# First layer of a four-layer graph stack: two fp32 products become three rounded passes each, with their inputs split by ScalarE and VectorE

## The chip, the cores and the metric

The kernel runs on one core of one Trainium2 chip. The metric is the device time of one execution in microseconds; the kernel before has a median of 2340.16 us over 3 runs (2339.61 to 2341.25).

## The reference

Input `x` is 128 graphs of 64 nodes with 256 features, 8192 token rows; `adj` is one 64 x 64 matrix that all graphs share. Four graph layers follow one another, each as `x = layernorm(x + layer(x, adj))`. The change touches the first. For it the reference, cut to its arithmetic, is:

```python
z  = (2 / lambda_max * L - I) @ x          # mixes the 64 nodes of a graph
h  = layernorm(z @ Wc + bc, g1, be1)
x1 = x + relu(h)
q, k, v = x1 @ Wq, x1 @ Wk, x1 @ Wv        # 4 heads of 64
a  = softmax(where(adj > 0, q @ k.T / 8, -1e9))
x2 = layernorm(x1 + (a @ v) @ Wo + bo, g2, be2)
m  = gelu(x2 @ W1 + b1) @ W2 + b2
x  = layernorm(x + layernorm(x2 + m, g3, be3))
```

The first product is `z @ Wc`, the output product `(a @ v) @ Wo`, both 256 x 256 weights.

## The kernel before, in words

The first layer runs over 32 groups of 256 token rows (`GROUP`), each as two tiles of 128 rows. Four groups are under way at once, the streams s0 to s3 (`STREAMS`); each stream has two PSUM banks, in two halves, and its own buffers. Each stream takes 8 turns, a new group each.

The work on a group is cut into numbered slots, each on one or several engines. In the texts here **s2.4** is slot 4 of stream 2. What the slots are, with the line of the trace that shows them:

- 0: TensorE mixes the nodes (L864, 4 matmuls of fp32, 128 columns); ScalarE copies the result out of PSUM as fp32 (L720).
- 1: TensorE's first product with Wc (L829, 4 fp32 matmuls of 256 columns, which a trace shows as 8 records); VectorE adds the bias (L777) and takes layernorm statistics (L319, L323); GpSimd makes the reciprocal root (L331, L333).
- 2: VectorE normalizes (L361 twice, L366 twice), and makes x1 (L784).
- 3: TensorE transposes x1 (L852), ScalarE writes its rounded upper part (`fm[s][:, 0]`, type fp32r, L723), VectorE the rest, the difference (`fm[s][:, 1]`, L767). This pair of instructions is a split.
- 4, 5: TensorE's products for q, k and v. Each fp32 product is made of three rounded passes (`exact_mm`, L298): upper by upper, rest by upper, upper by rest; 24 passes in slot 4, 12 in slot 5. ScalarE copies the results out (L726, L727, L730).
- 6: TensorE's scores (L883, L893), VectorE's maximum (L788). 7: ScalarE's exponentials (L734). 8: VectorE's sum and division (L792, L794, L796). 9: TensorE transposes (L900), ScalarE copies (L739). 10: attention by values (L911), ScalarE's copy (L742).
- 11: the output product with Wo (L829), VectorE's sum (L801) and statistics. 12: VectorE normalizes (L361, L366). 13: transposes, ScalarE's upper part (L746), VectorE's split (L767). 14: TensorE's 24 passes with W1; ScalarE's gelu (L750).
- 15: product with W2 (L829, 8 fp32 matmuls), VectorE's sum (L810) and statistics. 16: VectorE normalizes. 17: statistics for the last layernorm. 18: ScalarE applies it (L351). GpSimd adds on 512-element rows in 3, 13 and 16 (L703, L707, L711).

Every engine works through its queue in the order in which its instructions are written. That order comes from a table by hand, `plan0`: per engine and slot a tick. A turn of a stream starts `lead[s]` ticks earlier than that of stream 0, and a round is 88 ticks; `weave` goes through the ticks of a round and, at equal ticks, through the streams in order. Ticks only order the work, they are no times. The round is unrolled at both ends and stands in a loop between them. In one round every slot of every stream is done once, each at its own turn.

The layer is preceded by a setup, in which ScalarE and GpSimd also split the weights that the passes use (L505, L499), while VectorE and TensorE square a matrix of 64 x 64 step by step to find its largest eigenvalue. All engines meet at a barrier behind the setup, and again behind the layer.

Of the kernel before, what the change touches and what calls it, by code (L numbers as in the profile page):

```python
# [21 lines left out]
ALU = mybir.AluOpType  # L22
# [100 lines left out]
def build_program(nc, ctx, t, out_rows):  # L123
# [485 lines left out]
    xr0, zt_words, hbuf, x1, vt, x1b, x2b = ([buf(G2) for _ in S] for _ in range(7))  # L609
# [5 lines left out]
    zT_f = [blocks_of(v) for v in zt_words]  # L615
# [43 lines left out]
    with nc.Block() as block:  # L659
# [98 lines left out]
        def _(dve):  # L758
# [65 lines left out]
        def _(pe):  # L824
# [7 lines left out]

            def product_by_graph(out, src, w):
# [974 lines left out]
```

## Time and profile before

| | us |
|---|---|
| median of 3 runs | 2340.16 |
| profiled execution | 2342.6 |
| its span, first to last instruction | 2340.7 |
| first layer, first to last of its matmuls | 42.4 to 674.2 |
| one round of the first layer | 78.40 |

The page gives shares over the whole program, of which the first layer is a quarter; what bounds it is read in stretches and timelines of that layer. Since one round is like the next, one of them is shown, from s2.4 at 219.24 us to s2.4 at 297.66 us. A row of a timeline merges instructions of one line that follow one another. The rows are in the section ahead of the prediction.

### The profile page before, as it was taken

Reading aid. Unit: us, or ns where it says so; the run is one execution under the profiler, and the core shown is the slowest. Engines: PE = TensorE matmul, PEld = TensorE weight load, DVE = VectorE, ACT = ScalarE, POOL = GpSimd, SP = SyncE. Lnnn points to the kernel's source line nnn. Section 1 sums busy time; section 2 is a strip of 40 time slices with the busy share of each in tenths; the row PEclk is TensorE's granted clock in tenths of the full one; section 3 lists DMA queues with packets and bytes.
Section 4 is the critical chain, followed back from the end, with each engine's and each line's share of the span. In section 5 each row is a group of like instructions: output and inputs, shape, how many; then the busy total and the mean of one; then the engine's idle time right before and its main releaser. Section 6 shows DMA issues by size and latency. Waiting matters only on the chain. (4 is left out here: it accounts for less than half of the span.)

```text
span 2340.7 us, 39332 instructions
## 1 busy us (share of the span) xinstructions
PE 2172.1 (93%) x14671; PEld 1939.7 (83%) x14671; DVE 1391.9 (59%) x2733; ACT 1206.5 (52%) x2295; POOL 480.1 (21%) x905
## 2 busy tenths in 40 slices
PE   5999999999969989999999999999998897979997
PEld 3888888888859988888888889988887897968886
DVE  3788778877855645443334433444433787857776
ACT  1453455345523347644444434444433566958887
POOL 3344334433430000000000000000000221016665
PEclk9999999999979999999999999999999898989999
DMA  2110111011122101000000000000000331012221
GB/s 97 33 55 18 40 49 54 18 40 49 37 82 63 54 30 36 1 18 1 1 1 19 19 1 1 1 1 1 1 1 18 107 109 54 0 32 64 72 72 50
DMA packets 76397, 81.77 MB, mean 35 GB/s; under 512 B 6545, under 2 KB 74001, under 8 KB 75409
## 3 DMA queue, kind: packets, MB, share of 16 engines
q1 hardware_dynamic: 76304, 80.51, 10.9%
q8 instruction: 62, 1.02, 0.2%
q14 instruction: 31, 0.25, 0.0%
HBM read 55.33 MB, written 25.17 MB: 34 GB/s over the span
## 5 line engine op out<-in xcount | busy, mean ns | idle before, releaser
L298 PE MATMUL ps<-R 128*128 128x256 f32 (+3 forms) x8520 | 1490.9, 335 | 38.2 <-DVE R L1506 14.2
L298 PEld LDWEIGHTS ps<-R 128*128 128x128 f32 x8520 | 1326.6, 190 | 183.2 <-DVE R L767 14.8
L1200 ACT ACTIVATE late_half<-ps,lstm_bias 128x512 f32<-128x512 f32 (+2 forms) x460 | 283.0, 669 | 383.0 <-PE ps L298 382.9
L340 POOL TENSOR_TENSOR ln_veps<-ln_mv,eps_tile 128x2 f32<-128x2 f32 x128 | 28.4, 222 | 1283.0 <-DVE ln_mv L323 1283.0
L829 PE MATMUL ps<-H 128*128 128x256 f32 x1024 | 237.6, 381 | 3.0 <-ACT H L750 1.7
L829 PEld LDWEIGHTS ps<-H 128*128 128x128 f32 x1024 | 189.0, 191 | 26.1 <-ACT H L750 1.9
L1235 DVE TENSOR_TENSOR late_half<-late_half 128x1024 f32<-128x1024 f32 (+2 forms) x32 | 37.6, 1175 | 186.8 <-ACT late_half L1200 186.8
L1197 ACT ACTIVATE late_half<-late_half 128x1024 f32<-128x1024 f32 (+2 forms) x66 | 68.1, 1031 | 124.4 <-DVE late_half L1240 78.4
L1237 DVE TENSOR_TENSOR late_half<-late_half 128x1024 f32<-128x1024 f32 (+2 forms) x32 | 37.6, 1175 | 132.6 <-ACT late_half L1200 132.6
L366 DVE SCALAR_TENSOR_TENSOR H<-H,ln_rstd 128x256 f32<-128x256 f32 x192 | 106.5, 596 | 6.7 <-POOL ln_rstd L333 3.2
L319 DVE BATCH_NORM_STATS2 ln_stats<-H 128x6 f32<-128x256 f32 x256 | 95.9, 416 | 5.3 <-POOL H L711 2.0
L1244 DVE TENSOR_TENSOR H<-late_half 128x1024 f32<-128x1024 f32 (+2 forms) x34 | 45.8, 1348 | 89.2 <-ACT late_half L1200 89.2
L1219 DVE TENSOR_TENSOR R<-H,R 128x1024 fp32r<-128x1024 f32 (+2 forms) x66 | 95.6, 1450 | 1.3 <-ACT R L1180 1.1
L343 POOL TENSOR_TENSOR ln_rstd<-ln_veps,minus_half 128x2 f32<-128x2 f32 x128 | 92.9, 726 | 10.0
L1180 ACT ACTIVATE R<-H 128x1024 fp32r<-128x1024 f32 (+2 forms) x66 | 94.4, 1432 | 0.0
L361 DVE SCALAR_TENSOR_TENSOR H<-H,ln_mv 128x256 f32<-128x256 f32 x192 | 90.6, 512 | 2.2 <-issue 1.8
L1247 DVE TENSOR_TENSOR late_half<-late_half 128x1024 f32<-128x1024 f32 (+2 forms) x32 | 37.6, 1176 | 81.1 <-ACT late_half L1200 81.1
L750 ACT ACTIVATE H<-ps,b_col 128x256 f32<-128x256 f32 x128 | 50.2, 474 | 66.1 <-PE ps L298 66.1
L1025 PE MATMUL ps<-adjT,H 128*128 128x128 f32 x512 | 61.0, 281 | 21.4 <-DMA H<-residual 21.4
L1025 PEld LDWEIGHTS ps<-adjT,H 128*128 128x128 f32 x512 | 60.2, 198 | 21.7 <-issue 21.7
L323 DVE BATCH_NORM_AGGREGATE ln_mv<-ln_stats 128x2 f32<-128x6 f32 x448 | 56.0, 166 | 35.2 <-DVE ln_stats L319 27.9
L331 POOL TENSOR_TENSOR ln_veps<-ln_mv,eps_tile 128x2 f32<-128x2 f32 x96 | 21.5, 224 | 268.9 <-DVE ln_mv L323 268.9
(208 smaller groups left out, 2860.6 us busy)
## 6 DMA issues: line engine op xcount, KB each, us to landing
H<-in_x SPq DMA_DIRECT2D x64, 256.0 KB, 4.1
residual<-H SPq DMA_DIRECT2D x32, 256.0 KB, 2.2
H<-residual SPq DMA_DIRECT2D x32, 256.0 KB, 2.9
arena<-residual SPq DMA_DIRECT2D x32, 256.0 KB, 2.7
residual<-arena SPq DMA_DIRECT2D x32, 256.0 KB, 2.2
H_state<-residual SPq DMA_DIRECT2D x32, 256.0 KB, 2.7
out<-H_state SPq DMA_DIRECT2D x32, 256.0 KB, 2.2
arena<-in_wih SPq DMA_DIRECT2D x4, 1024.0 KB, 5.0
```

What stands on the lines that cost most here:

```text
L298: mm = pe.matmul(out, lhsT(a), rhs(b), start=start and n == 0, stop=stop and n == len(PASSES) - 1)
L319: c.step(dve.bn_stats(ln_stats[:, s, n, :], y[:, n, :]))
L323: ins = dve.bn_aggr(ln_mv[:, s, n, :], ln_stats[:, s, n, :])
L343: c.step(pool.tensor_tensor(ln_rstd[:, s, :], ln_veps[:, s, :], minus_half[:, 0:TILES], ALU.pow))
L361: c.step(dve.scalar_tensor_tensor(out=y[:, n, :], in0=y[:, n, :], scalar=ln_mv[:, s, n, 0:1], in1=g, op0=ALU.subtract, op1=ALU.mult))
L366: ins = dve.scalar_tensor_tensor(out=y[:, n, :], in0=y[:, n, :], scalar=ln_rstd[:, s, n:n + 1], in1=be, op0=ALU.mult, op1=ALU.add)
L829: mm = pe.matmul(out[:, n, :], src[:, k, n * P:(n + 1) * P], w[:, k, :], start=(k == 0), stop=(k == blocks - 1))
L1025: mm = pe.matmul(out[:, k, n * P:(n + 1) * P], src[:, n, k * P:(k + 1) * P], adjT[:], start=True, stop=True)
L1180: act.activation(x.as_window(xin[x.s][:, 0]), x.window(), ACT.Copy).then_inc(x_hi[x.s], 1)
L1197: act.activation(x.part(bg), x.part(cell[s]), ACT.Tanh).then_inc(tanh_ready[s], 1)
L1200: ins = act.activation(into[q][:, m, 0:x.cols], gate_ps(q, m, x.cols), ACT.Tanh if q == TANH_G else ACT.Sigmoid, bias=lstm_bias[:, x.p - 1 ...
L1219: dve.tensor_tensor(x.as_window(xin[x.s][:, 1]), x.window(), x.as_window(raw(xin[x.s][:, 0])), ALU.subtract).then_inc(x_ready[x.s], 1)
```

## The change

- The weights Wc and Wo get split copies `Wc_r` and `Wo_r` in `R`; the setup splits six weights instead of four.
- The buffers for the fp32 copies (`zt_words`, `zT_f`) go. In slots 0 and 10 ScalarE writes the upper part into `fm[s][:, 0]`, the pair that slots 3 and 13 use, and VectorE makes the rest. So VectorE has four splits for a group instead of two.
- The products of slots 1 and 11 are `exact_product`: per product 12 passes instead of 4 fp32 matmuls. The product with W2 in slot 15 stays in fp32.
- Slots 1 and 11 wait for the split (`fm_ready`) instead of the copy.
- In `plan0` VectorE gets ticks for slots 0 and 10, and several ticks move by one or two.

```diff
-    splits0 = ((Wq_r, Wq), (Wk_r, Wk), (Wv_r, Wv), (W1_r, W1))
+    splits0 = ((Wc_r, Wc), (Wq_r, Wq), (Wk_r, Wk), (Wv_r, Wv), (W1_r, W1), (Wo_r, Wo))
...
-    FM = 2
+    FM = 4
     plan0 = dict(
         period=88, lead=(0, 13, 19, 31),
-        pe={0: 15, 1: 19, 3: 31, 4: 36, 5: 41, 6: 46, 9: 60, 10: 65, 11: 70, 13: 80, 14: 86, 15: 93},
-        act={0: 18, 3: 34, 4: 39, 5: 44, 7: 54, 9: 64, 10: 67, 13: 81, 14: 89, 18: 122},
-        dve={1: 26, 2: 31, 3: 35, 6: 51, 8: 60, 11: 77, 12: 80, 13: 85, 15: 100, 16: 104, 17: 111},
+        pe={0: 13, 1: 19, 3: 31, 4: 36, 5: 41, 6: 46, 9: 60, 10: 64, 11: 71, 13: 81, 14: 87, 15: 94},
+        act={0: 15, 3: 34, 4: 39, 5: 44, 7: 54, 9: 63, 10: 66, 13: 82, 14: 90, 18: 122},
+        dve={0: 17, 1: 26, 2: 31, 3: 35, 6: 51, 8: 59, 10: 68, 11: 77, 12: 80, 13: 86, 15: 101, 16: 104, 17: 111},
...
                 if slot == 0:
                     act.wait_ge(mixed[s], 2 * turn + 1)
-                    act.activation(zT_f[s], feature_major(s, 0), ACT.Copy).then_inc(mixed_ready[s], 1)
+                    act.activation(fm[s][:, 0], feature_major(s, 0), ACT.Copy).then_inc(fm_hi[s], 1)
...
                 if slot == 10:
                     act.wait_ge(mixed[s], 2 * turn + 2)
-                    act.activation(zT_f[s].rearrange("p k (n q) -> p n k q", n=TILES), mixed_rows(s),
-                                   ACT.Copy).then_inc(mixed_ready[s], 1)
+                    act.activation(tile_order(fm[s][:, 0]), mixed_rows(s), ACT.Copy).then_inc(fm_hi[s], 1)
...
+                if slot == 0:
+                    split_lo(s, FM * turn + 1, feature_major(s, 0), as_is)
+                if slot == 3:
+                    split_lo(s, FM * turn + 2, feature_major(s, 0), as_is)
+                if slot == 10:
+                    split_lo(s, FM * turn + 3, mixed_rows(s), tile_order)
+                if slot == 13:
+                    split_lo(s, FM * turn + 4, feature_major(s, 1), as_is)
...
+            def exact_product(out, src, w):
+
+                for n in range(TILES):
+                    for k in range(KD):
+                        mm = exact_mm(pe, out[:, n, :], lambda q: src[:, q, k, n * P:(n + 1) * P],
+                                      lambda q: w[:, q, k, :], k == 0, k == KD - 1)
+                return mm
...
                 if slot == 1:
-                    pe.wait_ge(mixed_ready[s], 2 * turn + 1)
-                    product(token_major(s, 1), zT_f[s], Wc).then_inc(product_done[s], 1)
+                    pe.wait_ge(fm_ready[s], FM * turn + 1)
+                    exact_product(token_major(s, 1), fm[s], Wc_r).then_inc(product_done[s], 1)
...
                 if slot == 11:
-                    pe.wait_ge(mixed_ready[s], 2 * turn + 2)
-                    product(token_major(s, 0), zT_f[s], Wo).then_inc(product_done[s], 1)
+                    pe.wait_ge(fm_ready[s], FM * turn + 3)
+                    exact_product(token_major(s, 0), fm[s], Wo_r).then_inc(product_done[s], 1)
```

In the changed file the lines have moved: L864 is L883, L829 is L840, L852 is L871, L298 is L299, L767 is L770, L319/L323/L361/L366 are one higher, L784 is L795, L792 to L796 are L803 to L807, L801 is L812.

**TensorE at the start of a round**, right behind the end of the loop. Before, the rows after the branch are s2.1, s3.3, s1.0, s0.15, s3.4, s1.1 (`ps<-H 128x256` are fp32 products, `ps<-R` the passes):

```order
L829 MATMUL ps<-H 128x256 x4
L852 MATMUL ps<-ident,H 128x2x64 x4
L864 MATMUL ps<-lnormT,H 128x128 x4
L829 MATMUL ps<-H 128x256 x8
L298 MATMUL ps<-R 128x256 x24
L829 MATMUL ps<-H 128x256 x4
```

Now they are s1.0, s2.1, s3.3, s3.4, s0.15, and s1.1 with s3.5:

```order
L883 MATMUL ps<-lnormT,H 128x128 x4
L299 MATMUL ps<-R 128x256 x12
L871 MATMUL ps<-ident,H 128x2x64 x4
L299 MATMUL ps<-R 128x256 x24
L840 MATMUL ps<-H 128x256 x8
L299 MATMUL ps<-R 128x256 x24
```

What moved: the passes of s3.4 now stand directly behind the transposes of s3.3, and the long product of s0.15 behind them instead of ahead; s1.0 stands first.

**VectorE in the middle of a round**, around the output product of stream 3. Before: s3.11 (its sum and statistics), s1.8 (sum, reciprocal, division), s3.12 (normalizing):

```order
L801 TENSOR_TENSOR H<-ps,H 128x512
L86 REGISTER_ALU
L319 BN_STATS ln_stats<-H 128x6 x2
L86 REGISTER_ALU
L323 BN_AGGR ln_mv<-ln_stats 128x2 x2
L792 TENSOR_REDUCE sm_sum<-H 128x8
L794 RECIPROCAL sm_inv<-sm_sum 128x8
L796 TENSOR_TENSOR H<-H,sm_inv 128x512
L359 REGISTER_ALU
L361 SCALAR_TENSOR_TENSOR H<-H,ln_mv 128x256 x2
```

Now s1.8, s3.11, the new split of s2.10 (`R<-ps,R 128x2x2x128`), s3.12:

```order
L803 TENSOR_REDUCE sm_sum<-H 128x8
L805 RECIPROCAL sm_inv<-sm_sum 128x8
L807 TENSOR_TENSOR H<-H,sm_inv 128x512
L810 REGISTER_ALU
L812 TENSOR_TENSOR H<-ps,H 128x512
L86 REGISTER_ALU
L320 BN_STATS ln_stats<-H 128x6 x2
L86 REGISTER_ALU
L324 BN_AGGR ln_mv<-ln_stats 128x2 x2
L770 TENSOR_TENSOR R<-ps,R 128x2x2x128
L360 REGISTER_ALU
L362 SCALAR_TENSOR_TENSOR H<-H,ln_mv 128x256 x2
```

What moved: s1.8 stands ahead of s3.11, and a split stands between s3.11 and s3.12.

**VectorE at the start of a round**, behind the branch. Before: s3.2, s1.16, s2.17, the split of s3.3:

```order
L361 SCALAR_TENSOR_TENSOR H<-H,ln_mv 128x256 x2
L366 SCALAR_TENSOR_TENSOR H<-H,ln_rstd 128x256 x2
L784 SCALAR_TENSOR_TENSOR H<-H 128x512
L361 SCALAR_TENSOR_TENSOR H<-H,ln_mv 128x256 x2
L366 SCALAR_TENSOR_TENSOR H<-H,ln_rstd 128x256 x2
L319 BN_STATS ln_stats<-H 128x6 x2
L323 BN_AGGR ln_mv<-ln_stats 128x2 x2
L767 TENSOR_TENSOR R<-ps,R 128x512
```

Now s3.2, s1.16, the new split of s1.0, s2.17, the split of s3.3:

```order
L362 SCALAR_TENSOR_TENSOR H<-H,ln_mv 128x256 x2
L367 SCALAR_TENSOR_TENSOR H<-H,ln_rstd 128x256 x2
L795 SCALAR_TENSOR_TENSOR H<-H 128x512
L362 SCALAR_TENSOR_TENSOR H<-H,ln_mv 128x256 x2
L367 SCALAR_TENSOR_TENSOR H<-H,ln_rstd 128x256 x2
L770 TENSOR_TENSOR R<-ps,R 128x512
L320 BN_STATS ln_stats<-H 128x6 x2
L324 BN_AGGR ln_mv<-ln_stats 128x2 x2
L770 TENSOR_TENSOR R<-ps,R 128x512
```

What moved: one split more ahead of that of s3.3. A second one, of s2.0, stands in the same queue just ahead of the branch, behind the split of s0.13.

## Rows read from the trace of the kernel before

**Rows 1.** The page: its first line, and busy time by engine.

```profile
span 2340.7 us, 39332 instructions
...
PE 2172.1 (93%) x14671; PEld 1939.7 (83%) x14671; DVE 1391.9 (59%) x2733; ACT 1206.5 (52%) x2295; POOL 480.1 (21%) x905
```

**Rows 2.** Stretches: length; busy us of PE, PEld, DVE, ACT, POOL; clock; DMA share; GB/s.

```profile
219.20:297.60 78.40, 73.20 (x712) 66.82 (x712) 63.65 (x153) 37.02 (x90) 32.64 (x53) 1.00 0.13 40
297.60:376.00 78.40, 73.20 (x712) 66.82 (x712) 63.66 (x154) 37.03 (x90) 32.65 (x53) 1.00 0.13 40
...
611.20:690.00 78.80, 57.98 (x577) 52.27 (x575) 54.11 (x129) 35.34 (x86) 30.66 (x51) 0.91 0.15 48
```

**Rows 3.** TensorE's timeline of one round: start us, us, line, tiles, records, idle before.

```profile
219.24 3.13 PE L298 MATMUL ps<-R 128*128 128x256 f32 x24 [1.66 <-DVE R L767]
223.78 0.66 PE L852 MATMUL ps<-ident,H 128*128 128x128 f32 x4 [1.41 <-DVE H L784]
...
246.35 0.66 PE L852 MATMUL ps<-ident,H 128*128 128x128 f32 x4 [0.92 <-DVE H L366]
...
249.29 3.12 PE L298 MATMUL ps<-R 128*128 128x256 f32 x24
252.25 1.89 PE L829 MATMUL ps<-H 128*128 128x256 f32 x8
253.98 0.60 PE L900 MATMUL ps<-ident,H 128*128 128x128 f32 x4
...
282.45 0.61 PE L852 MATMUL ps<-ident,H 128*128 128x128 f32 x4
...
283.79 3.62 PE L829 MATMUL ps<-H 128*128 128x256 f32 x16
287.06 3.21 PE L298 MATMUL ps<-R 128*128 128x256 f32 x24
...
297.66 0.39 PE L298 MATMUL ps<-R 128*128 128x256 f32 x1 [1.67 <-DVE R L767]
```

**Rows 4.** Who waited for whom in that round, TensorE: us in total, times, longest.

```profile
PE ps L852 <- DVE H L784: 2.0, 3, 1.4
PE ps L298 <- DVE R L767: 1.7, 1, 1.7
```

**Rows 5.** VectorE's timeline of the same round.

```profile
220.01 2.98 DVE L366 SCALAR_TENSOR_TENSOR H<-H,ln_rstd 128x256 f32<-128x256 f32 x2
...
241.17 0.69 DVE L801 TENSOR_TENSOR H<-ps,H 128x512 f32<-128x512 f32 x1 [1.40 <-PE ps L829]
...
242.97 0.65 DVE L792 TENSOR_REDUCE sm_sum<-H 128x8 f32<-128x512 f32 x1
...
245.41 0.88 DVE L366 SCALAR_TENSOR_TENSOR H<-H,ln_rstd 128x256 f32<-128x256 f32 x2
...
271.55 0.69 DVE L810 TENSOR_TENSOR H<-ps,H 128x512 f32<-128x512 f32 x1 [2.18 <-PE ps L829]
...
285.12 0.66 DVE L767 TENSOR_TENSOR R<-ps,R 128x512 fp32r<-128x512 f32 x1
285.70 0.68 DVE L777 TENSOR_TENSOR H<-ps,H 128x512 f32<-128x512 f32 x1
```

**Rows 6.** ScalarE's timeline of the same round.

```profile
237.93 0.65 ACT L742 ACTIVATE H<-ps 128x512 f32<-128x512 f32 x1
...
240.41 1.75 ACT L734 ACTIVATE H<-ps,sm_max 128x64 f32<-128x64 f32 x8
...
278.06 0.60 ACT L720 ACTIVATE H<-ps 128x512 f32<-128x512 f32 x1 [3.75 <-PE ps L864]
```

**Rows 7.** The line of the split: ns shortest/median/longest, first and last start.

```profile
L767 DVE TENSOR_TENSOR R<-ps,R x64: 655/690/693, 55.2 to 663.9; 128x512 fp32r<-128x512 f32 x64
```

**Rows 8.** Timeline of the setup, GpSimd's weight splits and VectorE's last step.

```profile
27.05 6.01 POOL L499 TENSOR_TENSOR R<-H,R 128x512 fp32r<-128x512 f32 x4 [6.36 <-ACT R L505]
...
40.31 0.60 DVE L576 TENSOR_SCALAR bg_rows<-ps,arena 128x64 f32<-128x64 f32 x2
```

More of the change, by code:

```diff
@@ L232, in build_program @@
     W1_r = w0r(2, KD, HID0)
+    Wc_r, Wo_r = (w0r(2, KD, D) for _ in range(2))
     buf = region(H_words, H2_words[:, 0:KD * TOKENS - W0_WORDS])
     xs = [buf(G2) for _ in range(STREAMS)]
-    splits0 = ((Wq_r, Wq), (Wk_r, Wk), (Wv_r, Wv), (W1_r, W1))
+    splits0 = ((Wc_r, Wc), (Wq_r, Wq), (Wk_r, Wk), (Wv_r, Wv), (W1_r, W1), (Wo_r, Wo))
     wg = region(arena[:])
@@ L606, in build_program @@
     end_phase()
-    xr0, zt_words, hbuf, x1, vt, x1b, x2b = ([buf(G2) for _ in S] for _ in range(7))
+    xr0, hbuf, x1, vt, x1b, x2b = ([buf(G2) for _ in S] for _ in range(6))
     attn = [buf(HEADS * TILES, NODES) for _ in S]
@@ L614, in build_program @@
     y_t = x2b_t
-    zT_f = [blocks_of(v) for v in zt_words]
     fm = [w0r(2, KD, GROUP) for _ in S]
@@ L632, in by_graph, with tile_order @@
         return v.rearrange("p k (g n i) -> p k n g i", g=2, n=TILES)
+    def tile_order(v):
+        return v.rearrange("p k (n q) -> p n k q", n=TILES)
     def graph_rows(g):
@@ L639, in up_ps @@
             "p (m n) -> p m n", m=HID0 // P)
-    (xr0_loaded, mixed, mixed_ready, product_done, turned, fm_hi, fm_ready,
+    (xr0_loaded, mixed, product_done, turned, fm_hi, fm_ready,
      var_ready, rstd_ready, x_ready, biased_ready, qkv_done, qkv_ready, sc_done, sc_ready, exp_ready, at_ready,
      atT_ready, up_done, gelu_ready, var2_ready, rstd2_ready, y_made, yx_ready, y_ready, y_stored) = (sems(n) for n in
-                  ("xr0_loaded", "mixed", "mixed_ready", "product_done", "turned",
+                  ("xr0_loaded", "mixed", "product_done", "turned",
                    "fm_hi", "fm_ready", "var_ready", "rstd_ready", "x_ready", "biased_ready",
@@ L762, in _, with split_lo, as_is @@
             ahead(dve, var2_ready, by=2)
-            def split_lo(s, count, half):
+            def split_lo(s, count, source, order):
                 dve.wait_ge(fm_hi[s], count)
-                dve.tensor_tensor(fm[s][:, 1], feature_major(s, half), raw(fm[s][:, 0]), ALU.subtract)\
+                dve.tensor_tensor(order(fm[s][:, 1]), source, order(raw(fm[s][:, 0])), ALU.subtract)\
                    .then_inc(fm_ready[s], 1)
+            def as_is(v):
+                return v
             def stage(s, slot, turn):
                 c = (steps if slot < 15 else tail).enter(s, slot, turn)
-                for n, (at, h) in enumerate(((3, 0), (13, 1))):
-                    if slot == at:
-                        split_lo(s, FM * turn + n + 1, h)
+                if slot == 0:
[6 more added lines that the diff above has]
+                    split_lo(s, FM * turn + 4, feature_major(s, 1), as_is)
                 if slot == 1:
@@ L873, in stage @@
                 if slot == 4:
-                    pe.wait_ge(fm_ready[s], FM * turn + 1)
+                    pe.wait_ge(fm_ready[s], FM * turn + 2)
                     product_T(feature_major(s, 0), Wq_r, fm[s], KD)
@@ L922, in stage @@
                 if slot == 14:
-                    pe.wait_ge(fm_ready[s], FM * turn + 2)
+                    pe.wait_ge(fm_ready[s], FM * turn + 4)
                     product_T(up_ps(s), W1_r, fm[s], HID0 // P).then_inc(up_done[s], 1)
```

## The prediction

> **What bounds the kernel now.** I read the page first: TensorE is busy 93% of the span [rows 1]. The first layer, the only part that the change touches, then went through the view of stretches. It repeats with a period of 78.40 us: the step s2.4 starts at 219.24 and again at 297.66 [rows 3], and in every full round TensorE is busy 73.20 us and VectorE 63.66 us [rows 2]. The reader is to see two things there: TensorE idles 78.40 - 73.20 = 5.20 us a round, and VectorE 78.40 - 63.66 = 14.74 us. Next I read TensorE's own timeline: it has no idle time from 249.29 to 282.45, but it waits 1.41 us at s1.3, 0.92 us at s3.13 and 1.67 us at s2.4 [rows 3], every time for VectorE; the view of waits gives the first as L852 after VectorE's L784, and the last as L298 after L767 [rows 4]. So the round is bound by TensorE in its middle, and by VectorE from s2.15 at 271.55 to s2.4: VectorE's nine steps from there to the end of the split of s3.3 take 285.12 + 0.66 - 271.55 = 14.2 us with almost no gap [rows 5], and TensorE is there at 287.06, only 1.3 us later [rows 3]. A step that is put into VectorE's queue in that stretch is paid nearly in full; so is one that waits.
>
> **The change, part by part.**
>
> *The products.* Per round eight products (s0.1 to s3.1, s0.11 to s3.11) go from four fp32 matmuls to twelve passes. The fp32 product s1.11 takes 253.98 - 252.25 = 1.73 us; twenty-four passes (s3.14) take 252.25 - 249.29 = 2.96 us, so twelve take 1.48 us [rows 3]. Gain: 0.25 us each, 8 x 0.25 = 2.0 us a round of TensorE time, at most 16 us over eight rounds, and of use only where TensorE bounds. The Trainium skill (FP8 and Floating Point Precision, TensorE Precision Notes) says that true FP32 takes four passes through the array; three instead of four would make a product 1.73 x 3/4 = 1.30 us and save 3.4 us a round. The rows of passes that already run here do not agree, at 1.48 us.
>
> *The copies.* ScalarE writes the upper part into the shared pair in the place of the old fp32 copy, same shape, 0.6 us [rows 6]: nothing.
>
> *The new splits.* VectorE gets eight more instructions a round like those of L767, which take 655 to 693 ns [rows 7]; followed by other work one occupies 285.70 - 285.12 = 0.6 us [rows 5]. That is 8 x 0.6 = 4.8 us a round: it would fit into 14.74 us of idle time, if it fell there. Each also puts a VectorE step between copy and product, and as VectorE works in order, the wait for a copy holds what is queued behind it. I went round once, in the order of the changed tables, with durations from rows, from s2.4 at 219.24 (before) on:
>
> 1. s0.0's split stands between s2.3 and s1.2. s1.2 runs into two GpSimd additions (its L366 pair takes 2.98 us instead of 0.88 [rows 5]), so 0.3 to 0.6 of the 0.6 us shows: s1.3 starts at 224.35 instead of 223.78. The faster s0.1 gives 0.1 back; +0.5.
>
> 2. s3.10's split comes right after s0.3's. Its copy starts at 237.93 [rows 6], now some 0.6 later, and ends at 239.15; VectorE, free since 236.7, waits 2.4 us for it and s1.6 and s2.8 stand behind. TensorE meanwhile does s0.4, and s3.11 starts at 239.9 instead of 239.24; +0.6 to 0.7.
>
> 3. s1.8 now stands ahead of s3.11. It needs the exponentials of s1.7, which ended at 240.41 + 1.75 = 242.16 [rows 6] and now end at 242.7. Before, s3.11 started at 241.17 and s3.12 ended at 246.29, with s1.8 between: 1.80 + 3.32 = 5.12 us [rows 5]. Now s1.8, s3.11, the new split of s2.10 (0.6) and s3.12 follow 242.7: 5.12 + 0.6 = 5.7, so s3.13 starts at 248.5 instead of 246.35 [rows 3]; +2.2.
>
> 4. s3.13's split now stands behind s1.10's, whose copy ends at 250.35: s3.14 starts at 251.7 instead of 249.29; +2.4. From here to s2.15 TensorE runs nearly without idle time; s*.11 gives back 0.25 twice, s2.13 and s3.0 take 0.3: s2.15 ends 2.2 later, at 273.7.
>
> 5. From 273.7 VectorE has the same 14.2 us to the end of s3.3's split, plus the splits of s2.0 and s1.0 (1.2), plus about 1.0 of waiting: s2.0's copy, which started at 278.06 [rows 6], now starts at 279.95 and VectorE is free at 279.6; less the gaps that fill, 15.9 us in all. End: 289.6.
>
> 6. **The two TensorE steps that change places.** Before, s3.3 (282.45) is followed by s1.0 and s0.15 (3.27 us from 283.79), and only then by s3.4 at 287.06 [rows 3]. Now s3.4 is straight behind s3.3. TensorE arrives at 286.0 and waits for the split until 289.65, about 3.6 us; s0.15 comes after that, from 292.6 to 296.05 plus 0.2 to its last result. VectorE's s0.15 (also moved, behind s2.2) can't start before 296.25, and s0.15, s1.1, s0.16 and s2.3's split (1.8 + 1.8 + 1.7 + 0.65) end at 302.2 or 302.3. So s2.4 starts at about 302.3 instead of 297.66. Of these 4.7 us VectorE's own delay at the split of s3.3 makes 289.6 - 285.78 = 3.8, which would come through even if s0.15 had kept its place; the exchange adds 0.9.
>
> The round becomes 302.3 - 219.24 = 83.1 us, +4.7. Bounds by the terms: without the exchange's 0.9, without the 1.0 of waiting in item 5 and with the smaller end of item 1 (0.3 less), +2.5; with one more collision with a GpSimd addition of the kind of item 1 in each half, 2 x 1.0, +6.7. I take 83.1, since each of its steps is a wait whose both ends are in rows.
>
> *Sum.* Seven full rounds from the first s2.4 to the last: 7 x 4.7 = 32.9. In the draining stretch (611.2 on, where TensorE is busy only 57.98 of 78.80 us [rows 2]) items 1 to 4 hold, 5 and 6 have no next turn: +2.2. The fill has each stream's first product one VectorE step later, two of them exposed: +1.5 (0 to 3). The weights' two more splits on GpSimd before the layer: four take 6.01 us from 27.05, so with two more of 1.3 GpSimd ends at 35.6; VectorE's last setup step ends at 40.91 [rows 8], so it is covered; its small additions can collide with GpSimd a little longer, +0.6 (0 to 1.3). Sum: 32.9 + 2.2 + 1.5 + 0.6 = 37.2. The profiled execution took 2342.6 us (span 2340.7), which is 2.4 us above the median of 2340.16; 2342.6 + 37.2 = 2379.8 on its scale and 2377.4 against the median. **Forecast 2377 us.** Low end of the terms 7 x 2.5 + 1.5 = 19, 2359 us; high end 7 x 6.7 + 2.2 + 3 + 1.3 = 53.4, 2394 us.
>
> **The rivals.**
>
> *A, TensorE bounds and the splits are hidden (faster).* For it: 93% busy and 14.74 us of idle VectorE a round. Then the round is 78.4 - 2.0 = 76.4 and the time 2340 - 16 = 2324; by the page's four passes against three, 2340 - 27 = 2313. Against it: TensorE's waits in every round are all for VectorE [rows 4], and half of the new splits lie where VectorE has no gap. It decides if VectorE's split of s3.3 ends before TensorE is through with s3.3, which needs 3.6 us less on VectorE. Chance 0.09.
>
> *B, the splits cost their own time only (slower, less).* The four splits in VectorE's dense stretch (s3.0, s2.0, s1.0, s0.0; 2.4 us a round) are paid, the moved steps find slack: 8 x (2.4 - 1.0) = 11, 2351 us; with item 5's wait of 1.0 us too, 2359. For it: before, TensorE came 1.3 us later than the split of s3.3 was ready, so there is some slack. Against it: s0.15's 3.27 us, which made that slack, is what moved away. Chance 0.14, with a further 0.03 that it nets to nothing (within 5 us of 2340).
>
> *C, the waits feed each other (slower, more).* VectorE and TensorE wait for each other twice a round (s0.15's product, s3.11's), and every later VectorE step can meet a GpSimd addition, which stretched a pair of L366 by 2.1 us [rows 5]. Three such meetings more would be 7 x (4.7 + 3) + 4 = 58, 2398 us. Chance 0.08.
>
> That the change doesn't do what it says is not among them: the built order has the passes and the splits.
>
> **How the numbers follow.** Forecast 0.66, A 0.09, B 0.14, nothing 0.03, C 0.08. From 2354 to 2396 lie the forecast with the ends of its terms, half of B's and a part of C's cases, about 8 in 10; that is the range. About 0.2% (4.7 us) is what a measurement of this kernel can tell from no change: faster 0.09, same 0.03, slower 0.88.
>
> **What would show it.** In the new profile a round of 83 us; TensorE's longest wait some 3.6 us, at the passes of s3.4 after the turning of s3.3, for VectorE's L770; a wait of about 2.2 us at s3.13's transposes; VectorE waiting some 2 us for ScalarE's copy of s3.10 and 1 us for that of s2.0; products of 1.48 us; splits of 0.6 to 0.7 us; a layer 37 us longer and all that follows unchanged. The prediction is wrong if the round is near 76 us, with TensorE's waits no longer than before (then VectorE had more room than its order shows), or if the passes with new operands run at another pace than 123 ns each.

## The result and the profile after

| | before | after |
|---|---|---|
| median, us (4 runs each) | 2339.89 (2339.42 to 2341.25) | 2393.90 (2393.85 to 2394.24) |
| ratio, 95% interval | | 1.023 (1.0212 to 1.0248) |
| span of the profiled execution, us | 2340.7 | 2392.0 |

The change makes the kernel 54.0 us slower; 37 were forecast, between 14 and 56. The page of the changed kernel, to be laid beside [rows 1]:

```profile
span 2392.0 us, 39966 instructions
...
PE 2184.9 (91%) x14927; PEld 1960.5 (82%) x14927; DVE 1426.8 (60%) x2797; ACT 1209.2 (51%) x2297; POOL 490.0 (20%) x907
```

VectorE has 1426.8 - 1391.9 = 34.9 us more busy time, for 64 more splits. TensorE, whose work should have become less, has 12.8 us more busy time and 38.5 us more idle time. Where this lies is read round by round. The first layer's s2.4 starts at 66.20, 150.55, 236.29, 321.17, 406.90, 490.24, 577.68 and 660.82 us: seven rounds of 84.35, 85.74, 84.88, 85.73, 83.34, 87.44 and 83.14 us. Before, the seven from s2.4 at 64.42 to s2.4 at 610.72 were 76.11, 78.71, 78.42, 78.38, 78.40, 78.40 and 77.88 us. The last two, in the view of stretches (length; busy us of PE, PEld, DVE, ACT, POOL; clock; DMA share; GB/s):

```profile
490.24:577.68 87.44, 77.41 (x744) 71.95 (x744) 68.15 (x161) 37.14 (x91) 33.92 (x53) 0.92 0.12 36
577.68:660.82 83.14, 72.33 (x744) 66.98 (x744) 67.86 (x161) 37.26 (x91) 33.88 (x53) 1.00 0.13 38
```

The two rounds hold the same instructions. The second ran at a granted clock of 1.00 and took 83.14 us; the forecast for a round was 83.1. The first had a mean clock of 0.92 and took 4.30 us more, with 5.08 us more busy time for TensorE. So there are two things to explain, the round at full clock and the slow stretches. First the full-clock round in TensorE's timeline, the rows that answer to [rows 3]:

```profile
577.68 3.14 PE L299 MATMUL ps<-R 128*128 128x256 f32 x24 [1.04 <-DVE R L770]
582.86 0.66 PE L871 MATMUL ps<-ident,H 128*128 128x128 f32 x4 [2.04 <-DVE H L795]
583.27 6.00 PE L299 MATMUL ps<-R 128*128 128x256 f32 x48
...
607.08 0.66 PE L871 MATMUL ps<-ident,H 128*128 128x128 f32 x4 [1.86 <-DVE H L367]
610.40 4.58 PE L299 MATMUL ps<-R 128*128 128x256 f32 x36 [0.41 <-DVE R L770]
...
648.12 3.15 PE L299 MATMUL ps<-R 128*128 128x256 f32 x24 [3.27 <-DVE R L770]
660.82 0.39 PE L299 MATMUL ps<-R 128*128 128x256 f32 x1 [1.04 <-DVE R L770]
```

They are s2.4, s1.3, the passes behind it, s3.13, s3.14, s3.4 and the next s2.4. The wait at s3.4 is new, those at s3.13 (0.92 before) and s1.3 (1.41 before) are longer, that at s2.4 (1.67 before) is shorter, and all are for VectorE. VectorE's timeline of the same round shows its own new waits:

```profile
597.72 0.69 DVE L770 TENSOR_TENSOR R<-ps,R 128x512 fp32r<-128x512 f32 x1 [2.40 <-ACT R L746]
...
609.06 1.29 DVE L770 TENSOR_TENSOR R<-ps,R 128x512 fp32r<-128x512 f32 x2 [1.44 <-ACT R L746]
...
632.38 0.69 DVE L821 TENSOR_TENSOR H<-ps,H 128x512 f32<-128x512 f32 x1 [0.97 <-PE ps L840]
...
639.23 0.69 DVE L770 TENSOR_TENSOR R<-ps,R 128x512 fp32r<-128x512 f32 x1 [0.79 <-ACT R L724]
...
647.41 0.66 DVE L770 TENSOR_TENSOR R<-ps,R 128x512 fp32r<-128x512 f32 x1
...
654.76 0.69 DVE L821 TENSOR_TENSOR H<-ps,H 128x512 f32<-128x512 f32 x1 [1.46 <-PE ps L840]
```

These are the split of s3.10, those of s1.10 and s3.13, the sum of s2.15, the splits of s2.0 and s3.3, and the sum of s0.15.

Now the slow stretches, in the 87.44 us round: the 48 passes behind s1.3, s3.13's transposes and s3.4, and then the clock in stretches from the middle of s3.4's wait (559.33 to 562.71) on:

```profile
495.83 7.48 PE L299 MATMUL ps<-R 128*128 128x256 f32 x48
...
520.28 1.12 PE L871 MATMUL ps<-ident,H 128*128 128x128 f32 x4 [1.88 <-DVE H L367]
...
562.71 5.42 PE L299 MATMUL ps<-R 128*128 128x256 f32 x24 [3.38 <-DVE R L770]
```

```profile
559.00:562.70 3.70, 0.33 (x4) 0.09 (x1) 3.42 (x11) 1.57 (x3) 1.27 (x1) 0.78 0.17 59
562.70:566.00 3.30, 3.29 (x15) 3.29 (x16) 2.97 (x11) 0.00 (x0) 1.40 (x4) 0.50 0.04 14
566.00:568.10 2.10, 2.10 (x12) 2.10 (x11) 1.81 (x4) 0.00 (x0) 1.94 (x4) 0.54 0.00 0
568.10:572.00 3.90, 3.90 (x22) 3.49 (x21) 0.38 (x1) 1.09 (x2) 1.06 (x1) 1.00 0.00 0
```

The clock fell while TensorE waited for VectorE, was 0.50, the 1.2 GHz level, for the passes of s3.4, which took 5.42 us instead of 3.15, and was back at 2.4 GHz from 568.10 on. The same 48 passes took 7.48 us here and 6.00 us in the next round.

Set against the rounds of before one by one, the seven took 8.2 + 7.0 + 6.5 + 7.4 + 4.9 + 9.0 + 5.3 = 48.3 us more. The two that ran at a clock of 1.00 are the fifth, 4.94 us more than the fifth before, and the last, 5.26 more. An estimate from this: at full clock all seven would take 7 x 4.94 = 34.6 us more, and the slow stretches have the other 13.7 us. (The 12.6 us in an expectation below is the sum over seven rounds of 83.14 us; it leaves out that the first round, as before, is shorter than the others.)

The account, in the profiled executions: the first s2.4 starts 1.8 us later (66.20 against 64.42; 0.6 of it is a later start of the layer), the rounds take 34.6 us more at full clock and 13.7 more by the slow stretches, and from the last s2.4 to the first matmul of the second layer it is 90.36 us instead of 84.86, 5.5 us more. Sum: the second layer starts 55.6 us later. At the end of the program 51.3 us of this are left, and the medians differ by 54.0.

### The profile page after: what moved, and what is told of

It reads as the page before. It is cut to its first block and busy times, and to the rows that moved or that the text cites. A ratio compares the mean times of both kernels' runs of the same rounds, so it can differ in the third digit from the quotient of the medians.

```text
span 2392.0 us, 39966 instructions
## 1 busy us (share of the span) xinstructions
PE 2184.9 (91%) x14927; PEld 1960.5 (82%) x14927; DVE 1426.8 (60%) x2797; ACT 1209.2 (51%) x2297; POOL 490.0 (20%) x907
## 5 line engine op out<-in xcount | busy, mean ns | idle before, releaser
L299 PE MATMUL ps<-R 128*128 128x256 f32 (+3 forms) x9288 | 1603.7, 333 | 63.6 <-DVE R L770 37.7
L299 PEld LDWEIGHTS ps<-R 128*128 128x128 f32 x9288 | 1435.8, 193 | 213.3 <-DVE R L770 45.5
L770 DVE TENSOR_TENSOR R<-ps,R 128x512 fp32r<-128x512 f32 x128 | 86.1, 683 | 67.1 <-ACT R L746 39.8
L840 PE MATMUL ps<-H 128*128 128x256 f32 x512 | 116.9, 381 | 1.7 <-ACT H L753 1.7
L840 PEld LDWEIGHTS ps<-H 128*128 128x128 f32 x512 | 96.0, 193 | 13.7 <-ACT H L753 1.9
L362 DVE SCALAR_TENSOR_TENSOR H<-H,ln_mv 128x256 f32<-128x256 f32 x192 | 99.9, 560 | 0.7
L367 DVE SCALAR_TENSOR_TENSOR H<-H,ln_rstd 128x256 f32<-128x256 f32 x192 | 92.1, 521 | 8.5 <-POOL ln_rstd L334 5.3
L753 ACT ACTIVATE H<-ps,b_col 128x256 f32<-128x256 f32 x128 | 50.2, 475 | 82.3 <-PE ps L299 82.3
```

The source lines that it names most:

```text
L299: mm = pe.matmul(out, lhsT(a), rhs(b), start=start and n == 0, stop=stop and n == len(PASSES) - 1)
L362: c.step(dve.scalar_tensor_tensor(out=y[:, n, :], in0=y[:, n, :], scalar=ln_mv[:, s, n, 0:1], in1=g, op0=ALU.subtract, op1=ALU.mult))
L367: ins = dve.scalar_tensor_tensor(out=y[:, n, :], in0=y[:, n, :], scalar=ln_rstd[:, s, n:n + 1], in1=be, op0=ALU.mult, op1=ALU.add)
L770: dve.tensor_tensor(order(fm[s][:, 1]), source, order(raw(fm[s][:, 0])), ALU.subtract)\
L840: mm = pe.matmul(out[:, n, :], src[:, k, n * P:(n + 1) * P], w[:, k, :], start=(k == 0), stop=(k == blocks - 1))
```

## The experiments

The kernel before took 2339.26 us beside the first four kernels below, 2339.28 us beside the next four and 2340.88 us beside the last three.

**Undoing the moves in the table, in the changed kernel.** First the exchange of s0.15 and s3.4 alone:

```diff
-        pe={... 13: 81, 14: 87, 15: 94},
+        pe={... 13: 81, 14: 87, 15: 93},
```

> The changed kernel (2393.9 us) with one tick put back: TensorE's slot 15 at 93, so that the product s0.15 stands ahead of the passes of s3.4 again. Theory, order and clock: s3.4's wait of 3.38 us falls to about 0.3, the round without a slow stretch goes from 83.14 to about 82.2 us, and the stretches at half clock behind that wait, 12.6 us over seven rounds, go: about 2374 us. Rival, the splits cost their own time whatever the order: the wait turns up at another place and the time stays within 5 us of 2394.

Measured: 2371.58 us (ratio to before 1.0134, 1.0117 to 1.0151), 22.3 us less than the changed kernel. TensorE's timeline, s0.15, then s3.4 (24 of the 48 passes, with s1.1 and s3.5 behind them), s2.4 and, one round on, s2.4 again:

```profile
460.44 3.62 PE L840 MATMUL ps<-H 128*128 128x256 f32 x16
463.95 6.02 PE L299 MATMUL ps<-R 128*128 128x256 f32 x48
...
475.02 4.64 PE L299 MATMUL ps<-R 128*128 128x256 f32 x24 [1.96 <-DVE R L770]
...
557.20 3.13 PE L299 MATMUL ps<-R 128*128 128x256 f32 x24 [1.96 <-DVE R L770]
```

s0.15 is back ahead of s3.4, and s3.4's wait is gone altogether. What is left of the loss has moved on: s2.4 now waits 1.96 us for VectorE instead of 1.04. From s2.4 to s2.4 a round takes 79.9 us for the first and 81.5 to 83.4 for the others, so the exchange is worth at least 83.3 - 81.5 = 1.8 us a round. The other half of the theory missed: the slow stretches did not go. Every one of the seven rounds has a mean clock of 0.94 to 0.98, and in four of them s2.4's passes, behind the wait of 1.96 us, took 4.28 to 4.64 us instead of 3.13. That the time came within 3 us of the expectation is in part luck: a round shorter than forecast, and slow stretches that stayed.

Then s1.8 back behind s3.11 alone:

```diff
-        dve={... 6: 51, 8: 59, 10: 68, ...},
+        dve={... 6: 51, 8: 60, 10: 68, ...},
```

> The changed kernel with VectorE's slot 8 at tick 60, so that s1.8 stands behind s3.11 again. Theory, order: s3.13's wait of 1.88 us falls to about 1.1 and the round to about 82.4 us; s3.4's wait and the half clock behind it stay: about 2389 us. Rival, the splits alone: no difference, 2394.

Measured: 2389.53 us (1.0208, 1.0191 to 1.0225). s3.13's wait went from 1.88 to 1.49 us:

```profile
432.60 0.66 PE L871 MATMUL ps<-ident,H 128*128 128x128 f32 x4 [1.49 <-DVE H L367]
...
473.85 5.49 PE L299 MATMUL ps<-R 128*128 128x256 f32 x24 [3.37 <-DVE R L770]
```

Both together:

> Both ticks of the last two runs put back in the changed kernel. Theory, order: the two effects add, round about 81.5 us without half clock, 2368 to 2370 us, still some 28 us above the kernel before, which is what the splits cost by themselves. Rival, the splits alone: 2394. If order were all, it would come to 2340 or less.

Measured: 2366.44 us (1.0111, 1.0094 to 1.0128), 27.5 us less than the changed kernel. 22.3 + 4.4 would be 26.7, so the two add up. As in the first of the two runs s3.4 does not wait and s2.4 waits 1.96 us; its passes took 3.13 us behind four of these waits and 4.6 us behind three. A round takes 80.9 to 83.0 us, after a first of 78.1, and in each but the first the mean clock is still 0.96 or 0.98. Half of the loss is undone by two ticks; the other half is not.

**The idle time ahead of the slow clock.** TensorE gets 24 passes on weights alone, whose result is overwritten, in the place of s3.4's wait; everything else is as in the changed kernel:

```diff
                 if slot == 4:
+                    if s == 3:
+                        for n in range(24):
+                            pe.matmul(feature_major(s, 1)[:, 0, :], Wq_r[:, 0, 0, 0:P], Wk_r[:, 0, 0, :],
+                                      start=True, stop=True)
```

> The changed kernel, with 24 more passes of constants (a result that is overwritten, 2.95 us) in stream 3's slot 4 ahead of its wait, where TensorE idles 3.38 us in each round. They add work and take none away. Theory, that TensorE's clock falls because of that idle time: no half clock in s3.4, each round 83.1 us, 12 us less than the changed kernel in spite of 768 passes... that is, 192 more passes: about 2381 us. Rival, that the clock falls for another reason or that its cost is hidden: 2394 or more.

Measured: 2387.58 us (1.0204, 1.0187 to 1.0221), 6.3 us less instead of 13. The filler and s3.4, then s3.4's stretch and one behind s3.13:

```profile
473.74 2.91 PE L895 MATMUL ps<-R 128*128 128x256 f32 x23
477.15 3.14 PE L299 MATMUL ps<-R 128*128 128x256 f32 x24 [0.51 <-DVE R L770]
```

```profile
477.00:480.30 3.30, 3.15 (x25) 3.15 (x26) 2.97 (x12) 0.00 (x0) 1.26 (x4) 1.00 0.09 30
264.00:267.00 3.00, 2.76 (x39) 2.32 (x40) 0.78 (x2) 1.14 (x3) 1.26 (x1) 0.55 0.00 0
```

s3.4 ran at full clock in every round, where without the filler it had been slow in five of seven, so the slow clock there came from the idle time ahead of it. But in five of the rounds the slow clock now fell on two other places, s1.3 behind its wait of 2.04 us (in four of them its 48 passes show 7.47 to 7.49 us instead of 6.00, as in the row below) and s3.13 behind its wait of 1.88 us, and these rounds took 85.2 us. The profiled execution, 2390.59 us, was the slowest of the four.

```profile
239.78 7.49 PE L299 MATMUL ps<-R 128*128 128x256 f32 x48
```

The cause is shown for this place; that filling one wait wins the slow stretches back is refuted.

**The parts of the change apart.** The changed kernel with its splits, waits and order, but with fp32 products on an fp32 copy:

```diff
-                    exact_product(token_major(s, 1), fm[s], Wc_r).then_inc(product_done[s], 1)
+                    product(token_major(s, 1), zT_f[s], Wc).then_inc(product_done[s], 1)
...
-                    exact_product(token_major(s, 0), fm[s], Wo_r).then_inc(product_done[s], 1)
+                    product(token_major(s, 0), zT_f[s], Wo).then_inc(product_done[s], 1)
```

> The changed kernel with its table, its eight new VectorE instructions a round and TensorE's waits for them, but both products as four fp32 matmuls on ScalarE's unrounded copy, as in the kernel before: the splits and the order alone, without the passes. Theory, that the loss is the splits with their order: TensorE gets 2 us a round more, of which some 0.6 us is on the path: 2394 to 2400 us. Rival, that the passes with new operands, or the shared pair of buffers, are what costs: well below 2394, near 2340 to 2360.

Measured: 2397.57 us (1.0250, 1.0234 to 1.0267). The passes themselves give some 4 us in the changed kernel, hardly clear of noise (the intervals of the two ratios, 1.0234 to 1.0267 and 1.0212 to 1.0248, overlap); the loss is in splits and order.

The reverse, passes in both products, in the order of before:

```diff
-                if slot == 0:
-                    split_lo(s, FM * turn + 1, feature_major(s, 0), as_is)
...
-                if slot == 10:
-                    split_lo(s, FM * turn + 3, mixed_rows(s), tile_order)
...
-                    pe.wait_ge(fm_ready[s], FM * turn + 1)
+                    pe.wait_ge(fm_hi[s], 4 * turn + 1)
```

> The passes alone: both products as twelve passes, with the table of the kernel before and without the new splits; TensorE waits for the copy as before. The rest of the inputs is left out (the third pass uses the weights' rest a second time). Theory: 0.25 us a product, of which only the four products s*.11 lie where TensorE bounds, so about 1.0 us a round: 2340 - 8 = 2332 us. Rival, that all eight count: 2324. Rival, that the passes gain nothing in this place: 2340.

Measured: 2327.89 us (0.9951, 0.9938 to 0.9965), 11.4 us faster. A round in the view of stretches:

```profile
215.85:293.05 77.20, 71.08 (x744) 66.54 (x745) 63.66 (x153) 37.09 (x90) 32.75 (x53) 1.00 0.13 41
```

TensorE is busy 71.08 us instead of 73.20 [rows 2], 2.1 us less, as forecast (2.0), and 1.2 us of it shorten the round, where the expectation had 1.0. The time fell by 11.4 us, between the expectation (8) and the rival that all eight products count (16). That is all the change had to gain.

The first product alone in passes, with the changed order:

```diff
-        dve={0: 17, ... 8: 59, 10: 68, 11: 77, ...},
+        dve={0: 17, ... 8: 59, 11: 77, ...},
...
-                    exact_product(token_major(s, 0), fm[s], Wo_r).then_inc(product_done[s], 1)
+                    product(token_major(s, 0), zT_f[s], Wo).then_inc(product_done[s], 1)
```

> The changed kernel with its table, but the output product as before (fp32 matmuls on an unrounded copy, no split in slot 10): the first product's part alone. Its four splits all lie in VectorE's dense stretch, and s3.4 still stands ahead of s0.15. Theory: most of the loss stays, 2380 to 2388 us. Rival, that the splits of slot 10 in the middle of the round are half of the loss or more: 2367 or less.

Measured: 2394.29 us (1.0238, 1.0222 to 1.0253). The expectation missed: with neither the splits of slot 10 nor the output product's passes the loss is the same. s3.13 waits 1.62 us instead of 1.86 to 1.88, but s3.4 as long as before the edit:

```profile
220.68 3.13 PE L299 MATMUL ps<-R 128*128 128x256 f32 x24 [3.38 <-DVE R L771]
...
263.21 1.02 PE L870 MATMUL ps<-ident,H 128*128 128x128 f32 x4 [1.62 <-DVE H L367]
...
306.32 4.38 PE L299 MATMUL ps<-R 128*128 128x256 f32 x24 [3.37 <-DVE R L771]
```

The output product alone in passes, with the order of before nearly everywhere (here the first product's operands and waits are those of before, and the lines are set against the kernel before):

```diff
-        pe={... 9: 60, 10: 65, 11: 70, 13: 80, 14: 86, 15: 93},
-        act={... 9: 64, 10: 67, 13: 81, 14: 89, 18: 122},
-        dve={... 8: 60, 11: 77, 12: 80, 13: 85, ...},
+        pe={... 9: 60, 10: 65, 11: 71, 13: 80, 14: 86, 15: 93},
+        act={... 9: 63, 10: 67, 13: 81, 14: 89, 18: 122},
+        dve={... 8: 60, 10: 70, 11: 77, 12: 80, 13: 85, ...},
```

> The output product's part alone, and in another order: fp32 matmuls for the first product, twelve passes for the output product; the table of the kernel before, with VectorE's slot 10 at 70 (so that s3.10's split stands behind s1.6 and does not hold it), TensorE's slot 11 at 71 and ScalarE's slot 9 at 63. These four splits lie where VectorE has idle time and TensorE bounds. Theory: they are hidden, and the four products give 1.0 us a round: about 2333 us, faster than both kernels. Rival, that any split more costs time: 2345 or more.

Measured: 2344.63 us (1.0021, 1.0012 to 1.0030) in place of 2333. VectorE's split of s1.10, and TensorE's steps s0.9 and s2.13 behind it:

```profile
250.86 0.69 DVE L771 TENSOR_TENSOR R<-ps,R 128x512 fp32r<-128x512 f32 x1 [1.43 <-ACT R L747]
```

```profile
254.93 0.66 PE L918 MATMUL ps<-ident,H 128*128 128x128 f32 x4 [0.28 <-DVE H L806]
256.64 0.66 PE L870 MATMUL ps<-ident,H 128*128 128x128 f32 x4 [1.05 <-DVE H L367]
```

VectorE stands 1.43 us at one split, waiting for ScalarE's copy, with s2.11, s0.8 and s2.12 queued behind it. Whether that wait or the split itself costs was left to the next group.

**The order alone, and two other orders.** The kernel before with the changed table, without any new split and with its fp32 products:

```diff
-        pe={0: 15, ... 10: 65, 11: 70, 13: 80, 14: 86, 15: 93},
-        act={0: 18, ... 9: 64, 10: 67, 13: 81, 14: 89, 18: 122},
-        dve={... 8: 60, 11: 77, 12: 80, 13: 85, 15: 100, ...},
+        pe={0: 13, ... 10: 64, 11: 71, 13: 81, 14: 87, 15: 94},
+        act={0: 15, ... 9: 63, 10: 66, 13: 82, 14: 90, 18: 122},
+        dve={... 8: 59, 11: 77, 12: 80, 13: 86, 15: 101, ...},
```

> The kernel before's work (fp32 first and output products from the fp32 copies, two splits for a group), in the changed kernel's order: every tick of the changed table, without VectorE's entries for slots 0 and 10. Theory, the order costs by itself: s1.8 ahead of s3.11 makes s3.13 later by about 1 us, and s3.4 straight behind s3.3 makes TensorE wait there and s0.15 later, so a round of about 80.2 us instead of 78.4 and 2353 to 2360 us, some of it at the half clock. Rival, the order matters only together with the new splits: a round of 78.4 and 2340 us.

Measured: 2371.57 us (1.0134, 1.0118 to 1.0149), 30.7 us slower than before with the very same work. TensorE's timeline, s3.13, its next two steps, s3.4 and s2.4:

```profile
258.69 1.10 PE L852 MATMUL ps<-ident,H 128*128 128x128 f32 x4 [1.61 <-DVE H L366]
259.71 1.14 PE L911 MATMUL ps<-H 64*64 64x64 f32 x32
260.78 2.66 PE L829 MATMUL ps<-H 128*128 128x256 f32 x8
...
299.66 3.13 PE L298 MATMUL ps<-R 128*128 128x256 f32 x24 [1.41 <-DVE R L767]
...
312.64 3.14 PE L298 MATMUL ps<-R 128*128 128x256 f32 x24 [1.04 <-DVE R L767]
```

From s3.4 to s2.4 it is 12.98 us, where before it was 297.66 - 287.06 = 10.60 [rows 3]: s0.15 now stands between, and TensorE waits 1.41 us ahead of s3.4 with s0.15 ready behind it. In the middle, s3.13 waits 1.61 us instead of 0.92; VectorE's s3.12 now follows s3.11's statistics directly, without s1.8 between, and waits 0.27 us for GpSimd's reciprocal root as well. The two rounds at full clock took 80.78 us, 2.4 more than before (80.2 had been expected):

```profile
312.64:393.42 80.78, 73.65 (x713) 67.15 (x713) 62.88 (x153) 37.24 (x91) 34.27 (x52) 1.00 0.12 39
```

The first round, the shortest before too, took 80.42 us; four of the seven took 82.3 to 82.4, with the slow clock behind s3.13's wait, as the records of 1.10 and 1.14 us show (0.66 and 0.69 at full clock). Together the seven rounds took 571.4 us instead of 546.3: 25.1 us, of which 7 x 2.38 = 16.7 are at full clock and the rest, 8.4, is the slow clock's. The expectation held for the round, nearly, and missed the time by over 11 us, mostly by the clock.

The output product alone again, its split one tick later, behind s2.11:

```diff
-        dve={... 10: 70, 11: 77, ...},
+        dve={... 10: 71, 11: 76, ...},
```

> As the run with the output product alone in passes (fp32 first product, three splits for a group), with one difference: VectorE's split of the output product's input, slot 10, one tick later, and slot 11 one tick earlier, so that s1.10's split stands behind s2.11 and no longer waits for its copy ahead of it. Theory, that run's 2344.6 us was the wait of 1.43 us at this one place: a round of about 77.4 us and 2332 us, faster than the kernel before. Rival, the split's own 0.7 us four times a round is what costs: 2340 us or more.

Measured: 2340.57 us (0.9997, 0.9988 to 1.0006), 0.3 us from before. The wait of VectorE for the copy is gone, and TensorE's at s0.9 with it; that at s2.13 is unchanged:

```profile
252.01 0.66 DVE L771 TENSOR_TENSOR R<-ps,R 128x512 fp32r<-128x512 f32 x1
```

```profile
255.99 0.66 PE L870 MATMUL ps<-ident,H 128*128 128x128 f32 x4 [1.05 <-DVE H L367]
```

The split still stands ahead of s2.12, and in a round at full clock (s2.4 at 377.61) the sum of s2.11 starts 407.59 - 377.61 = 30.0 us behind s2.4, against 248.77 - 219.24 = 29.5 before. Such a round takes 78.7 us instead of 78.4. The theory that the one wait made the 2344.6 explains 4 of the 12 us that were missing. For the rest the trace points at the split's own time in a place where TensorE waits for VectorE (the 1.05 us at s2.13); no run took that away alone.

The whole work of the changed kernel, in an order near that of before:

```diff
-        pe={0: 13, ... 10: 64, 11: 71, 13: 81, 14: 87, 15: 94},
-        act={0: 15, ... 9: 63, 10: 66, 13: 82, 14: 90, 18: 122},
-        dve={0: 17, ... 8: 59, 10: 68, 11: 77, 12: 80, 13: 86, 15: 101, ...},
+        pe={0: 15, ... 10: 65, 11: 71, 13: 80, 14: 86, 15: 93},
+        act={0: 18, ... 9: 63, 10: 67, 13: 81, 14: 89, 18: 122},
+        dve={0: 19, ... 8: 60, 10: 71, 11: 76, 12: 80, 13: 85, 15: 100, ...},
```

> The whole work of the changed kernel (both products in passes, four splits for a group), in another order: the ticks of TensorE and ScalarE of the kernel before but for one each (ScalarE's slot 9, TensorE's slot 11), VectorE's slot 0 at 19, slot 8 at 60, slot 10 at 71, slot 11 at 76, slots 13 and 15 as in the kernel before. So s0.15 is ahead of s3.4 again, s1.8 behind s3.11, s1.0's split stands behind that of s3.3, and s2.0's behind s1.15's sum and statistics. Theory, most of the changed kernel's 54 us is its order: a round of about 78.6 us and 2336 to 2346 us. Rival, the four splits of slots 0 and 10 cost their own time wherever they stand in a busy queue: a round over 80.5 us and 2360 us or more.

Measured: 2350.86 us (1.0044, 1.0030 to 1.0058), between the two expectations: 43 us faster than the changed kernel with the same products and the same splits, and still 10 us slower than before. A round, and TensorE's two new waits in it, at s3.3 and s2.3:

```profile
223.84:303.83 79.99, 71.89 (x744) 66.66 (x744) 68.24 (x161) 37.16 (x90) 32.69 (x53) 1.00 0.12 39
```

```profile
287.94 0.66 PE L871 MATMUL ps<-ident,H 128*128 128x128 f32 x4 [0.84 <-DVE H L795]
...
299.76 0.66 PE L871 MATMUL ps<-ident,H 128*128 128x128 f32 x4 [1.09 <-DVE H L795]
```

TensorE's work is 1.3 us less than before a round, its idle time 2.9 us more: the split of s2.0 stands ahead of s3.2 on VectorE, and that of s1.0 ahead of s2.2. None of the kernels that compute everything is faster than the kernel before, and no order was tried beyond these, so a better one may exist.

**The account of the 54 us.** Along one path, each step a run: order alone +30.7 (1.0134), then the first product's passes and splits 1.0238 against 1.0134, some +24, then the output product's -0.4 (2393.90 against 2394.29), which is within noise. In rounds at full clock the same path is 78.40, 80.78, 83.45 to 83.50 and 83.34 us: 2.4 us for the order, 2.7 for the first product, nothing for the output product. The rest of the order's step holds 8.4 us of slow clock. In the better order the same first product costs 2350.86 - 2340.57 = 10.3, and the output product nothing. So the order costs 31 us by itself, and makes the first product, with its splits, 14 us dearer.

## Why the prediction was right, and where it was not

Direction, mechanism and the length of a round at full clock were right (83.1 forecast, 83.34 and 83.14 measured), and not by luck, as the offsets of the single steps show. Offsets from s2.4 in us, forecast as the numbers on record less 219.24, measured in the round from 577.68 (full clock) and in that from 490.24:

| step | forecast | full clock | with slow stretches |
|---|---|---|---|
| s1.3 (item 1) | 5.11 | 5.18 | 5.18 |
| s3.13 (item 3) | 29.3 | 29.40 | 30.04 |
| s3.14 (item 4) | 32.5 | 32.72 | |
| VectorE's sum of s2.15 (items 4, 5) | 54.5 | 54.70 | 56.51 |
| end of s3.3's split (item 5) | 70.4 | 70.39 | 72.41 |
| s3.4 (item 6) | 70.4 | 70.44 | 72.47 |
| VectorE's sum of s0.15 (item 6) | 77.0 | 77.08 | 81.38 |
| next s2.4 | 83.1 | 83.14 | 87.44 |

*The waits.* s3.10's split waits 2.40 us (forecast 2.4), s2.0's 0.79 (1.0), s3.4's 3.27 (3.6), s3.13's 1.86 (some 2.2). VectorE needs 70.39 - 54.70 = 15.7 us from s2.15's sum to the end of s3.3's split (15.9). That TensorE's waits before were "all" for VectorE is not quite so: 0.3 and 0.2 us a round were for ScalarE, which changes nothing in the sum.

*The products.* The gain in TensorE's time was forecast at 2.0 us a round, and 2.1 was measured with the passes alone. The Trainium skill (FP8 and Floating Point Precision, TensorE Precision Notes) has four passes for true FP32; the estimate of 3.4 us that three passes for four would give is not borne out by the 2.1.

*Put at nothing: TensorE's clock.* The sum has no term for it, and this is where most of the missing 17 us are: the slow stretches took some 13.7 us in the seven rounds. The rows shown ahead could not price it: before, waits of up to 1.67 us in every full round left the clock at 1.00 [rows 2]. Nor is the 0.91 of the stretch from 611.20 to 690.00 a sign of it: there the clock is 1.00 up to 674.30, with waits of 1.39 and 1.66 us among them, and falls only behind the layer's last matmul, where TensorE stands idle for 21.36 us:

```profile
674.30:678.00 3.70, 0.00 (x0) 0.00 (x0) 3.21 (x9) 0.00 (x0) 1.64 (x5) 0.78 0.21 71
678.00:690.00 12.00, 0.00 (x0) 0.00 (x0) 2.32 (x6) 3.24 (x5) 3.03 (x7) 0.50 0.38 131
```

*Mis-sized: the draining stretch.* Its "+2.2" measured 5.5. The prediction took TensorE to be busy only 57.98 of 78.80 us there, but all of the 57.98 lie in the 63.1 us up to 674.30, so it was 92% busy. And the clock is in it too, behind the waits of 2.03 us at s1.3 and of 2.28 us at s3.13:

```profile
666.40 7.48 PE L299 MATMUL ps<-R 128*128 128x256 f32 x48
...
693.37 7.88 PE L299 MATMUL ps<-R 128*128 128x256 f32 x48
```

The 48 passes took 7.48 and 7.88 us instead of some 6.0, 3.4 us together; how much of it other engines' work hides is not shown.

*The other terms.* The rounds at full clock, 7 x 4.7 = 32.9, measured 34.6 (4.9 a round); fill and setup, 1.5 + 0.6, measured 1.8. The layers behind the first, put at "unchanged", gave back 4.3. So the 37.2 of the sum become 34.6 + 13.7 + 5.5 + 1.8 - 4.3 = 51.3 us, the difference of the two spans.

*Wrong: what each move costs.* Item 6 gave 3.8 of the 4.7 us of a round to the splits in VectorE's queue, and 0.9 to the exchange of s0.15 and s3.4. With no new split at all, the new order makes a round at full clock 2.4 us longer, half of the 4.9, and undoing the exchange alone in the changed kernel gives at least 1.8 us a round and 22 us in all. There s3.4 does not wait at all, and what comes through stands at s2.4. The walk got the sum right, since both act at once there. The division into "would come through even if" was not walked, and it is the one statement of that part which the runs refute: it would have sent an engineer to the splits first, when two ticks alone were worth 27.5 us and a better order for all of them 43 us. The splits of slot 10 in particular, to which items 2 to 4 gave about half of the shift of s3.4, cost nothing in the changed kernel once their product's gain is counted (2394.29 without, 2393.90 with).

*The rivals.* A, hidden splits, was wrong: even in the best order tried the splits cost 23 us over the passes alone (2350.86 against 2327.89). B, splits at their own time only, is what the better order shows (2350.86; B said 2351): there the splits cost 79.99 - 77.20 = 2.8 us a round (B: 2.4) and the products give 1.2 (B: 1.0). It is not what the change did. C's 2398 us is near in size, but by another mechanism: TensorE's slow clock. A round has no more meetings with GpSimd than before: one pair of 3.02 us and one of 1.80, against 2.98 and 1.78.

*Open.* Which wait is followed by a slow stretch could not be told: the wait of 2.04 us at s1.3 was followed by one at 495.83 and not at 583.27. Why the layers behind the first give back 4.3 of the 55.6 us wasn't tried.

## What to carry to other kernels

Where two engines take turns waiting for each other, an operation moved off the bound engine onto the other is worth its time on the first only if the second has slack at that place; its idle time over a round says nothing. Test the order apart from the work: the old work in the new order, and the new work in the old order, are two cheap runs, and here the first alone was 31 of the 54 us. When a wait is gone, look where the next one is: undoing the exchange emptied s3.4's wait and lengthened s2.4's. And where a forecast puts new waits on TensorE like those here (1.5 to 3.4 us), add a term for its clock: 0 to 2.3 us for each.

## What the runs showed of the hardware

In the changed kernel TensorE is busy 87 to 90% of a round, and still it fell to the 1.2 GHz level behind single waits (0.50 in 562.70 to 566.00, behind 3.38 us; 0.52 in 258.60 to 261.60 of the run with the order alone, behind 1.61 us). In full rounds the shortest such wait was 1.49 us, in the run with both ticks put back, and not every wait did it: the same wait in the same place did in one round and not in the next. The wait of 1.66 us at s2.4, after which the profiled rounds of before show no slow stretch, was followed by one in a single round each of the passes alone, of both runs with the output product alone and of the better order (4.6 us for passes that take 3.13). Behind s3.4's wait the passes took 1.1 to 2.3 us longer, in five of seven rounds. In the changed kernel the slow stretches came to some 13.7 us in seven rounds, and with s3.4's wait filled they stood behind two others, of 2.04 and 1.88 us.

The new splits, which read PSUM, took 0.66 to 0.69 us also beside GpSimd's additions (that at 639.23 took 0.69, beside an addition from 639.03 to 640.33), while a pair of L362 on SBUF tiles beside them took 3.02 us:

```profile
490.70 3.02 DVE L362 SCALAR_TENSOR_TENSOR H<-H,ln_mv 128x256 f32<-128x256 f32 x2
```

The Trainium skill (SBUF — State Buffer, SBUF: two separate sides) says that a VectorE instruction with two SBUF inputs and a GpSimd one that reads SBUF lock each other out of a shared pair of ports. The 3.02 us for a pair that takes 0.88 alone [rows 5] agree, and so do the splits, whose first input is not in SBUF.
